# Logits of a router computed expert by expert and turned back, in a fused recurrent and mixture-of-experts block

## The reference, cut to what matters

```
xn = layernorm(x)
h  = rmsnorm(xn) * pre_norm_w                      # recurrent branch
a  = sigmoid(h @ w_a + bias); v = sigmoid(h @ w_i) * (h @ w_v)
rec = chunked_scan(a, sqrt(1 - a*a) * v)
y  = xn + rec @ out_proj_w
branch1 = y + (silu(h2 @ w_gate) * (h2 @ w_up)) @ w_down      # h2 = rmsnorm(y)*w
logits = xn @ w_router                             # (2048, 256) @ (256, 8)
top 2 of 8 experts, softmax over the two logits -> weights
branch2 = sum over the two experts of weight * square(relu(xn @ w_fc[e])) @ w_proj[e]
```

## Time and profile before

| what | value |
|---|---|
| median of 3 runs | 289.37 us (289.16 to 289.37) |
| profiled execution: its own time | 289.77 us |
| profiled execution: span of the core's work | 288.0 us |
| PE busy | 279.7 us, 97% of the span |
| PEld busy | 249.8 us, 87% |
| DVE / ACT / POOL busy | 202.4 / 170.8 / 145.7 us |
| granted clock of TensorE | 1.0 of full, every slice |

### The profile page before, as it was taken

One profiled execution on the slowest core, in us unless ns is written; L12 is line 12 of the kernel. 1 busy time (PEld: TensorE's weight loads), 2 busy tenths in 40 slices (PEclk: granted clock), 3 DMA queues, 4 the chain that ended last, 5 costly groups with the idle time before them and its releaser, 6 DMA issues.

```text
span 288.0 us, 5663 instructions
## 1 busy us (share of the span) xinstructions
PE 279.7 (97%) x1831; PEld 249.8 (87%) x1831; DVE 202.4 (70%) x467; ACT 170.8 (59%) x365; POOL 145.7 (51%) x138
## 2 busy tenths in 40 slices
PE   6999999999999999999999899999999999999995
PEld 5787988888988898898998789989989999888895
DVE  3896999999988978846458686545456554446973
ACT  3787868998849654435675545437477545432331
POOL 5498001244660126765777786756776776620000
PEclk9999999999999999999999999999999999999999
DMA  6999990016996011443344444344344535539922
GB/s 203 356 376 383 385 398 0 0 11 92 254 263 126 0 40 39 57 74 66 52 81 68 75 74 68 65 63 67 60 78 78 81 66 64 54 68 357 336 75 73
DMA packets 32584, 36.92 MB, mean 128 GB/s; under 512 B 4390, under 2 KB 29740, under 8 KB 32524
## 3 DMA queue, kind: packets, MB, share of 16 engines
q0 software_dynamic: 9616, 13.01, 27.9%
q1 hardware_dynamic: 20672, 21.31, 22.1%
q10 hardware_dynamic: 2268, 2.23, 2.2%
HBM read 24.68 MB, written 13.96 MB: 134 GB/s over the span
## 4 chain that ended last, share of the span: by engine, by line
PE 91%; ACT 3%; DVE 3%; issue 1%; POOL 1%; POOLq 0%; DVEq 0%; ACTq 0%
PE ps L396 76%; PE ps L642 6%; PE ps L465 5%; PE ps L400 2%; PE ps L478 1%; PE ps L411 1%; ACT hT_hi L790 1%; ACT X L775 1%; DVE Wpj_lo L1227 1%; ACT L817 0%; DVE dec L1098 0%; DVE hT_lo L1067 0%; ACT gain L817 0%; ACT gain L812 0%; PE ps L493 0%
## 5 line engine op out<-in xcount | busy, mean ns | idle before, releaser
L1527 POOL DMA_INDIRECT xg<-xh_dram,gather_u x39 | 46.6, 1194 | 47.4 <-DVE picks L1293 34.9
L1536 POOL DMA_INDIRECT acc_dram<-yb,gather_u x39 | 61.9, 1586 | 16.3 <-issue 8.9
L396 PE MATMUL ps<-h2T_lo,Wgu_hi 128*128 128x512 f32 (+1 forms) x132 | 42.8, 386 | 0.0
L396 PE MATMUL ps<-h2T_hi,Wgu_hi 128*128 128x512 f32 (+1 forms) x132 | 40.9, 391 | 0.0
L396 PE MATMUL ps<-h2T_hi,Wgu_lo 128*128 128x512 f32 (+1 forms) x132 | 40.1, 385 | 0.0
L1310 DVE TENSOR_TENSOR aT_lo<-ps,aT_hi 128x256 fp32r<-128x256 f32 x39 | 16.5, 424 | 28.2 <-ACT aT_hi L892 27.9
L396 PE MATMUL ps<-Wd_hi,guT_hi 128*128 128x256 f32 x128 | 36.3, 284 | 0.1
L396 PE MATMUL ps<-Wd_hi,guT_lo 128*128 128x256 f32 x128 | 36.2, 283 | 0.0
L396 PE MATMUL ps<-Wd_lo,guT_hi 128*128 128x256 f32 x128 | 36.1, 282 | 0.0
L1232 DVE TENSOR_TENSOR gu<-gu,ps 128x512 f32<-128x512 f32 x31 | 21.2, 684 | 13.2 <-PE ps L396 11.5
L850 ACT ACTIVATE gu<-ps 128x512 f32<-128x512 f32 x31 | 18.4, 593 | 20.3 <-PE ps L396 20.3
(11 more groups left out here) (189 smaller groups left out, 683.8 us busy)
## 6 DMA issues: line engine op xcount, KB each, us to landing
sums<-acc_dram SPq DMA_DIRECT2D x8, 512.0 KB, 7.8
acc_dram<-zero SPq DMA_DIRECT2D x1, 2176.0 KB, 14.5
Wgu_raw<-in_L_attn_w_gate_up_dram SPq DMA_DIRECT2D x4, 512.0 KB, 8.2
Wfc_raw<-in_L_ffn_w_fc_dram SPq DMA_DIRECT2D x4, 512.0 KB, 14.0
xh_dram<-X ACTq DMA_DIRECT2D x4, 512.0 KB, 7.7
Wpj_raw<-in_L_ffn_w_proj_dram SPq DMA_DIRECT2D x4, 512.0 KB, 9.1
X<-in_L_attn_x_dram SPq DMA_DIRECT2D x3, 512.0 KB, 6.9
out_dram<-X SPq DMA_DIRECT2D x3, 512.0 KB, 5.7
```

Source lines behind the costliest of these rows:

```text
L396: return nc.tensor.matmul(dst, lhs, rhs, start=start, stop=stop, skip_group_check=group)
L1527: pool.indirect_dma_start(out=xg[i % XG][:, :], out_offset=None, in_=xh_dram, in_offset=bass.IndirectOffsetOnAxis(ap=gather_u[:, i:i + 1], ...
L1536: pool.indirect_dma_start(out=acc_dram[i % 2], in_=yb[i % YB][:, :], in_offset=None, compute_op=ALU.add, out_offset=bass.IndirectOffsetOnA ...
```

## The change

The router becomes the stationary operand: for each k half, one product with 16 stationary columns and 512 moving columns of hT_hi, and one with 8 stationary columns and 512 of hT_lo. The result of a sequence is a bank with the experts on 16 partitions and the tokens along them. ACT copies it to `by_expert`; four small fp32 products with a constant of ones and zeros (`fold`) turn it back to tokens on partitions and add the two halves; DVE copies the 32 numbers per partition to `logit`. The bank is used again for each sequence, so `logits(c)` waits for DVE's copy of sequence c - 1. Further, ACT's split of sequence 2 is moved ahead of the norm of sequence 3.

```
@@ -152,6 +152,8 @@
         guT_at = room(8 * KB)
         gain = [put(f"gain{b}", [P, K, S], F32, at)
                 for b, at in enumerate((cum_at, cum_at, Wpj_hi_at + 8 * KB, Wpj_hi_at + 12 * KB))]
+
+        by_expert, fold = put("by_expert", [P, S], F32, guT_at), put("fold", [P, E], F32, guT_at + 2 * KB)
         guT = [(put(f"guT{u}_hi", [P, S], F32R, guT_at + 4 * KB * u),
                 put(f"guT{u}_lo", [P, S], F32R, guT_at + 4 * KB * u + 2 * KB)) for u in range(2)]
 
@@ -217,7 +219,9 @@
         xh_ready, xh_half = [sem(f"xh_ready{b}") for b in range(B)], sem("xh_half")
         xh_stored = [sem(f"xh_stored{b}") for b in range(B)]
         xT_done, hT_hi, hT_split, wr_hi, wr_split = sem("xT_done"), sem("hT_hi"), sem("hT_split"), sem("wr_hi"), sem("wr_split")
-        logit_done, logit_copied = sem("logit_done"), sem("logit_copied")
+        logit_done, logit_taken, logit_turned, logit_copied = (sem("logit_done"), sem("logit_taken"), sem("logit_turned"),
+                                                               sem("logit_copied"))
+        fold_ready = sem("fold_ready")
         tables_ready, q_ready = sem("tables_ready"), sem("q_ready")
         zero_row, zero_stored = sem("zero_row"), sem("zero_stored")
         x_copied = sem("x_copied")
@@ -417,15 +421,24 @@
                 pe.wait_ge(hT_split, K * (c + 1))
                 if c == 0:
                     pe.wait_ge(wr_split, 1)
+                else:
+                    pe.wait_ge(logit_copied, c)
+                for k in range(K):
+                    product(ps[0:2 * E, LOGIT, :], Wr_two[:, k, :, :].rearrange("p h e -> p (h e)"), hT[c][0][:, k, :],
+                            k == 0, False, True)
+                for k in range(K):
+                    last = product(ps[0:E, LOGIT, :], Wr_two[:, k, 0, :], hT[c][1][:, k, :], False, k == K - 1, True)
+                last.then_inc(logit_done, 1)
+
+            def turn_logits(c):
+
+                pe.wait_ge(logit_taken, c + 1)
+                if c == 0:
+                    pe.wait_ge(fold_ready, 1)
                 for j in range(J):
-                    t = J * c + j
-                    for k in range(K):
-                        rows_hi, rows_lo = (hT[c][h][:, k, j * P:(j + 1) * P] for h in range(2))
-                        product(ps[:, LOGIT, t * 2 * E:(t + 1) * 2 * E], rows_hi,
-                                Wr_two[:, k, :, :].rearrange("p h e -> p (h e)"), k == 0, False, True)
-                        last = product(ps[:, LOGIT, t * 2 * E:t * 2 * E + E], rows_lo, Wr_two[:, k, 0, :],
-                                       False, k == K - 1, True)
-                last.then_inc(logit_done, 1)
+                    last = nc.tensor.matmul(ps[:, LOGIT, j * E:(j + 1) * E], by_expert[0:2 * E, j * P:(j + 1) * P],
+                                            fold[0:2 * E, :], start=True, stop=True)
+                last.then_inc(logit_turned, 1)
 
             def aiv(b, n):
 
@@ -587,16 +600,20 @@
             transpose_x(1)
             aiv(0, 4)
             aiv(0, 5)
+            turn_logits(0)
             transpose_x(2)
             aiv(1, 0)
             logits(1)
             aiv(1, 1)
             transpose_x(3)
+            turn_logits(1)
             aiv(1, 2)
             logits(2)
             aiv(1, 3)
+            turn_logits(2)
             logits(3)
             aiv(1, 4)
+            turn_logits(3)
             output_projection(0, 0)
             output_projection(0, 1)
             aiv(1, 5)
@@ -793,6 +810,12 @@
                 act.wait_ge(router_loaded, 16)
                 A.activation(Wr_two[:, :, 0, :], Wr[:, :, :], ACT.Copy).then_inc(wr_hi, 1)
 
+            def take_logits(c):
+                act.wait_ge(logit_done, c + 1)
+                if c:
+                    act.wait_ge(logit_turned, c)
+                A.activation(by_expert[0:2 * E, :], ps[0:2 * E, LOGIT, :], ACT.Copy).then_inc(logit_taken, 1)
+
             def decay(b, r):
                 act.wait_ge(aiv_done, 6 * b + r + 1)
                 if b == 3:
@@ -918,18 +941,22 @@
             store_xh(0)
             input_gate(0, 0)
             input_gate(0, 1)
+            take_logits(0)
             split_h(1)
             store_xh(1)
             decay_squares(0)
             gains(0)
+            split_h(2)
             normalise_x(3)
             store_xh(2)
-            split_h(2)
             store_xh(3)
+            take_logits(1)
             split_h(3)
             decay(1, 0)
             decay(1, 1)
+            take_logits(2)
             weights_hi(3)
+            take_logits(3)
             input_gate(1, 0)
             input_gate(1, 1)
             decay_squares(1)
@@ -1114,14 +1141,17 @@
                                            in1=h2T[b % 2][0][:, k, :].bitcast(F32), op0=ALU.mult,
                                            op1=ALU.subtract).then_inc(h2T_split, 1)
 
-            def take_logits():
-                dve.wait_ge(logit_done, B)
-                two = ps[:, LOGIT, 0:2 * T * E].rearrange("p (t h e) -> p t h e", h=2, e=E)
-                chain.step(V.tensor_copy(logit[:, :, :], two[:, :, 1, :]))
-                V.tensor_tensor(logit[:, :, :], logit[:, :, :], two[:, :, 0, :], ALU.add).then_inc(logit_copied, 1)
+            def take_logits(c):
+                dve.wait_ge(logit_turned, c + 1)
+                V.tensor_copy(logit[:, J * c:J * (c + 1), :].rearrange("p t e -> p (t e)"),
+                              ps[:, LOGIT, 0:J * E]).then_inc(logit_copied, 1)
+
+            def fold_parts():
+                dve.wait_ge(consts_ready, 1)
+                V.tensor_tensor(fold[0:2 * E, :], ident[0:2 * E, 0:E], ident[0:2 * E, E:2 * E], ALU.add).then_inc(fold_ready, 1)
 
             def top_two():
-                dve.wait_ge(logit_copied, 1)
+                dve.wait_ge(logit_copied, B)
                 te = [P, T, E]
                 rank_te = rank8[:, None, :].to_broadcast(te)
                 work = logit
@@ -1318,6 +1348,7 @@
             gates_lo_first(1)
             split_h(0)
             statistics(1)
+            fold_parts()
             split_router()
             statistics(2)
             statistics(3)
@@ -1326,14 +1357,17 @@
             gated_value(0, 0)
             gated_value(0, 1)
             signal(0, 0)
+            take_logits(0)
             signal(0, 1)
             split_h(2)
             cumulate(0, 0)
+            take_logits(1)
             recur(0, 0)
             split_h(3)
             cumulate(0, 1)
+            take_logits(2)
             recur(0, 1)
-            take_logits()
+            take_logits(3)
             dve.wait_ge(tables_ready, 1)
             top_two()
             add_residual(0, 0)
```

More of the change, by code:

```diff
@@ L419, in logits, with turn_logits @@
                     pe.wait_ge(wr_split, 1)
-                for j in range(J):
[L421 to L428, removed]
+                else:
+                    pe.wait_ge(logit_copied, c)
+                for k in range(K):
+                    product(ps[0:2 * E, LOGIT, :], Wr_two[:, k, :, :].rearrange("p h e -> p (h e)"), hT[c][0][:, k, :],
+                            k == 0, False, True)
+                for k in range(K):
+                    last = product(ps[0:E, LOGIT, :], Wr_two[:, k, 0, :], hT[c][1][:, k, :], False, k == K - 1, True)
+                last.then_inc(logit_done, 1)
+            def turn_logits(c):
+                pe.wait_ge(logit_taken, c + 1)
+                if c == 0:
+                    pe.wait_ge(fold_ready, 1)
+                for j in range(J):
+                    last = nc.tensor.matmul(ps[:, LOGIT, j * E:(j + 1) * E], by_expert[0:2 * E, j * P:(j + 1) * P],
+                                            fold[0:2 * E, :], start=True, stop=True)
+                last.then_inc(logit_turned, 1)
             def aiv(b, n):
```

## The result

The changed kernel takes 290.6 us (median of 10 runs, 290.43 to 291.21) against 289.6 (median of 10, 289.16 to 290.21) for the kernel before: ratio 1.0036, 95% interval 1.0028 to 1.0044, or **1.0 us slower**. Forecast were 289.9, half a microsecond more than before, in a range of 288.5 to 291.1. The place and the direction of the shift were right. The size was half of what came: the forecast called it no measurable change (within 0.2%, or 0.58 us), and by that bound the changed kernel is slower.

The account below looks back on a forecast made before the run. PE's own list (busy 97%) was taken as the bound. Products and turns +0.36, old wait -0.5, new wait +0.75, small ones -0.1 made +0.5 us: 290.3 against the profiled 289.77, median 0.4 lower, so 289.9 us, range 288.5 to 291.1.

Parts of the forecast that it names:

- rival 2: Slower: plain fp32 instructions on PE don't overlap their loads; w up to 1.63, total up to 291.7 us, middle 290.6; 20%.
- Long products: PE's four products of 512 columns per call of logits: 0.23 us each, 0.92 a call, 0.78 less than before.
- The reordering: ACT's split of sequence 2 before the norm of sequence 3: transposes of sequence 3 start 1.31 us earlier, PE's 0.52 wait gone.
- rival 3: The reordering brings nothing: ACT isn't early, the transposes of sequence 3 stay at 27.33, total 291.1 us; 8%.
- The fourth transposes: PE's transposes of sequence 3, claimed to start at 26.02 instead of 27.33, without a wait.
- The price of a turn: On PE, turning one sequence's logits back: eight plain fp32 instructions at 0.109 us, 0.87 in all.
- w: PE's time for one turn, forecast 0.87 us; the output projection starts at 34.65 + 2w.
- ACT's second take: ACT's copy of sequence 1's logits, behind a store's issue: runs 26.33 to 26.92, so PE turns from 26.95.
- The new wait: PE stands still 0.75 us at logits(3), until DVE's copy of logits 2; DVE's chain takes 5.2 us.
- The end: Start of PE's output projection: 36.4 instead of 35.95, 0.5 us later, carried one to one to the kernel's end.
- rival 1: Turns on PE cost what the fp16 pairs cost, w = 0.25: output projection 0.8 us earlier, total 288.6 us; 15%.
- rival 4: DVE's chain isn't the limit, PE goes by its own work: logits(3) at 32.45, total 289.1 us; 12%.

Follow-up runs that it names:

- full rows: Changed kernel with the turning products over all 128 rows instead of 16, same values: 290.15 us, 0.5 under the changed kernel, ratio 1.0020 to the kernel before.

## Why the prediction was right, and what it missed

The measured 290.6 us lies in the stated range (288.5 to 291.1), but not in the narrower one of the forecast itself (289.4 to 290.4); it is the value named for the middle of rival 2. The median of before was 289.6 over ten runs instead of 289.37 over three, which makes 0.2 of the 0.7 us between forecast and result. The rest lies in the terms below.

- **Long products** at 0.23 each: 0.46 a pair, right. **`transpose_x(1)`** held by ACT's norm at 16.9: measured 16.97 on the scale of before (less the 0.21 of the late start), right.
- **The reordering** removing the old wait: right, and separately worth 0.7. The condition named in rival 3, that ACT must be early for it, was not needed.
- **The fourth transposes** at 26.02: measured 26.37. Of the 0.35, turn 0 with its edge makes 0.20, the start of `transpose_x(1)` 0.07 and the products behind the turn 0.08.
- **The price of a turn** is the term that was mis-sized: 0.87 forecast, 1.07 measured. The doubling to eight instructions was right, and so was the pitch: 0.109 forecast, 0.11 measured. Eight of them make 0.89; the other 0.18 are the edges, 0.08 ahead of the turn (20.87 to 20.95) and 0.10 by which the way to the transposes (20.95 to 21.94, 0.99) is longer than eight pitches. The prediction counted exposed loads at the turn among its small terms and made their sum -0.1. I had argued from a load's duration (178 ns for 6 rows, 190 for 128) that the rows filled don't matter. The duration is indeed nearly the same, but the load with 16 rows does not start ahead of its product. With full rows the turn takes 0.81, and 0.87 would have been enough.
- **Rival 2** gave w = 0.91 as the point from which the change is slower, and w came out at 1.07. The number is in its reach, its reason is not what happened: plain fp32 instructions do overlap their loads, at 0.11 each inside the turn, and with full rows at the edges too.
- **ACT's second take** as the limit of turn 1 was wrong in effect: the take ended at 26.65 + 0.59 = 27.24, as the issue of the store does hold ACT's list up (0.37 from 26.18, 0.50 idle), but PE came to the turn at 27.4 only and paid the edge instead. DVE stood 1.89 for the copy behind it, where 1.3 were forecast.
- **The new wait** at `logits(3)`: there, released by DVE's copy, 0.44 instead of 0.75. The chain on DVE was forecast at 5.2 us and is 5.22. What was missed is that the turn, being longer, reaches DVE at the same moment, so that the round trip binds too.
- **The end**: 36.4 for the output projection, 37.11 on the scale of before. Of the 0.7 between, 0.4 stand at the start of turn 1 already, 0.1 each are the length of turn 1, the edge of turn 3 and its length.
- **The other rivals**: turns at the price of the fp16 pairs (rival 1) fall with the pitch of 0.11. That PE's own work and not DVE's chain would decide (rival 4) is refuted by the 1.51 us of wait where the turns were made short. In the changed kernel itself the round trip and the chain ended together, so there it is half true. DVE kept up at `aiv(3,3)`, as forecast, and the shift reached the end one to one.

The plain fp32 loads of 128 columns last nearly alike, 186 ns on average with 16 rows (changed kernel) and 191 with 128 (full rows). The Trainium skill, TensorE: Matmul & The Clock Gate, section LDWEIGHTS (loading the stationary operand), has the time of a load go by its columns and not by the rows filled, and these rows agree. What differed is the overlap: loads of 128 rows started 0.22 us ahead of their product while another product of 128 rows was running, loads of 16 and of 64 rows did not (0.35 us idle behind a long product each time). The same page of the Trainium skill, section The mechanism, lets a load run ahead when its row group doesn't conflict with the running product's or when it goes to a background weight buffer. The loads of full rows fill every row that the running product uses, so of the two only the second can hold for them, though no row shows which buffer a load goes to. Why loads of fewer rows do not run ahead, no run here tells.

## What to carry to other kernels

Swapping the operands of many short products saves loads, but if the result must be turned back, count the instructions of that turn (two for each plain fp32 product, one for a transpose). Look at its edges too: with all 128 rows filled, a turn in plain fp32 between long products was 0.26 us shorter. Above all count the round trips. Four turns in plain fp32 with their hand-overs lost 1.6 us, one turn by transposes gained about 1.5 beside the reordering; between four turns and one, both by transposes, lie 2.1 to 2.4 us. Where two instructions of PE's list that need another engine in between are neighbours, PE pays the whole way there and back. And a split that another engine waits to continue goes ahead of work that is not needed so soon.

## What the runs showed of the hardware that was not expected

- Weight loads of 16 or 64 rows did not start ahead of their product; loads of 128 rows did, by 0.22 us. The same eight instructions took 1.07 us with 16 rows and 0.81 with 128, edges included; inside both turns they stood 0.11 apart.
- An fp32r load of 16 columns lasted 94 ns, one of 8 columns 88, of 64 columns 134, of 128 columns 188: it shrinks less than in proportion. Between products of 512 columns none of it was seen, the pairs stayed at 0.46 us.
- An issue of a transfer on ACT's queue held up the instruction behind it in ACT's list: the norm ended at 26.15, the issue took 0.37 from 26.18, and the take, whose inputs were ready, started at 26.65.
